# Five one-hot buffers, a peeled first pass, one block of counts turned per window, and weight splits between x1's low parts, in a two-layer graph kernel

## What is computed

```python
# layer 0, graph attention
h = x @ W
al, ar = h @ a_l, h @ a_r
e = exp(-leaky_relu(al[src] + ar[dst], 0.1))
h_prime = segment_sum(e[:, None] * h[dst], src) / (segment_sum(e, src)[:, None] + 1e-5)
x = layernorm(x + elu(h_prime))                       # called x1 below
# layer 1, relational convolution and gate
u = x @ root + bias
for r in range(8):
    mean = segment_sum(x[src] * (type == r), dst) / max(count, 1)
    u = u + mean @ weight[r]
z = concat([u, x]) @ w_gate + b_gate
out = layernorm(x + tanh(u) * z + x * (1 - z))
```

## Time and profile before

| what | us |
|---|---|
| median of 3 runs (1108.06 to 1109.21) | 1109.0 |
| the profiled execution, whole | 1109.11 |
| its span, first to last instruction | 1107.3 |
| TensorE busy in the span | 1042.9 (94%) |
| VectorE, ScalarE, GpSimd busy | 344.8, 275.4, 265.8 |
| mean granted TensorE clock | 0.977 of full |

### The profile page before, as it was taken

How to read it: one execution, slowest core, us unless ns; L and a number is a source line. 1 busy time by engine, 2 the same in 40 slices (tenths; PEclk the granted TensorE clock), 3 DMA queues, 4 the chain that set the end, 5 groups by cost and what they waited for, 6 DMA issues and landing times.

```text
span 1107.3 us, 14903 instructions
## 1 busy us (share of the span) xinstructions
PE 1042.9 (94%) x5430; PEld 857.2 (77%) x5430; DVE 344.8 (31%) x694; ACT 275.4 (25%) x470; POOL 265.8 (24%) x201
## 2 busy tenths in 40 slices
PE   5899879996999999999999999999999999999977
PEld 3566546775889889879889879889889889888855
DVE  7976765360112202202202102102102202112277
ACT  4322343383112212212212211211212211212320
POOL 0000000106331321221321321321321321327480
PEclk9999999998999999999999999999999998999989
DMA  6213335407321041041141141141141140212212
GB/s 209 76 39 108 94 96 152 133 28 262 122 76 39 30 147 37 29 146 37 31 145 38 29 146 30 38 145 34 33 146 38 30 147 28 75 48 67 76 39 92
DMA packets 63622, 91.81 MB, mean 83 GB/s; under 512 B 4116, under 2 KB 30179, under 8 KB 63429
## 3 DMA queue, kind: packets, MB, share of 16 engines
q1 hardware_dynamic: 63556, 90.86, 26.4%
HBM read 75.17 MB, written 15.67 MB: 82 GB/s over the span
## 4 chain that ended last, share of the span: by engine, by line
PE 84%; DVE 7%; POOL 3%; issue 3%; ACT 2%; DVEq 1%; DMA 0%; SPq 0%; ACTq 0%; POOLq 0%
PE ps L966 18%; PE ps L968 17%; PE ps L967 17%; PE ps L1154 9%; PE ps L1155 9%; PE ps L1030 4%; PE ps L993 2%; PE ps L1143 2%; DVE hot L790 2%; DVE oh_s L722 2%; POOL x_lo L426 1%; PE ps L1203 1%; POOL u L411 1%; PE ps L1205 1%; PE ps L1204 1%
## 5 line engine op out<-in xcount | busy, mean ns | idle before, releaser
L399 POOL TENSOR_TENSOR w_lo<-w_raw,w_hi 128x512 fp32r<-128x512 f32 x168 | 215.8, 1288 | 761.7 <-ACT w_hi L465 562.7
L966 PE MATMUL ps<-w_hi,M_hi 128*128 128x512 f32 (+1 forms) x560 | 223.4, 399 | 17.4 <-POOL w_lo L399 9.4
L465 ACT CAST w_hi<-w_raw 128x512 fp32r<-128x512 f32 x184 | 114.4, 622 | 498.2 <-PE ps L968 430.8
L968 PE MATMUL ps<-w_lo,M_hi 128*128 128x512 f32 (+1 forms) x560 | 219.7, 392 | 0.0
L967 PE MATMUL ps<-w_hi,M_lo 128*128 128x512 f32 (+1 forms) x560 | 219.7, 392 | 0.0
L883 DVE SCALAR_TENSOR_TENSOR u<-ps,scale,u 128x512 f32<-128x512 f32 (+1 forms) x90 | 66.4, 744 | 427.7 <-PE ps L968 427.7
L1154 PE MATMUL ps<-C_hi,x_hi 128*128 128x320 f32 (+3 forms) x640 | 194.0, 320 | 0.0
L1155 PE MATMUL ps<-C_hi,x_lo 128*128 128x320 f32 (+3 forms) x640 | 193.0, 318 | 0.0
L966 PE MATMUL ps<-w_hi,M 128*128 128x512 f32 (+1 forms) x360 | 142.9, 397 | 0.0
L967 PE MATMUL ps<-w_hi,M 128*128 128x512 f32 (+1 forms) x360 | 142.6, 396 | 0.0
L968 PE MATMUL ps<-w_lo,M 128*128 128x512 f32 (+1 forms) x360 | 142.3, 395 | 0.0
(11 more groups left out here) (145 smaller groups left out, 773.2 us busy)
## 6 DMA issues: line engine op xcount, KB each, us to landing
w_raw<-weights SPq DMA_DIRECT2D x192, 256.0 KB, 2.9
C_dram<-Cst SPq DMA_DIRECT2D x25, 512.0 KB, 6.0
C_hi<-C_dram SPq DMA_DIRECT2D x8, 1600.0 KB, 7.4
z<-b_gate SPq DMA_DIRECT2D x5, 512.0 KB, 9.8
u<-bias SPq DMA_DIRECT2D x5, 512.0 KB, 7.6
xT_raw<-xT SPq DMA_DIRECT2D x8, 312.5 KB, 7.5
u<-x SPq DMA_DIRECT2D x4, 512.0 KB, 5.2
out<-u SPq DMA_DIRECT2D x4, 512.0 KB
```

The lines of the kernel that those rows point to most:

```text
L399: pool.tensor_tensor(w_lo[k % RING][:, :], w_raw[k % RING][:, :], w_hi[k % RING][:, :].bitcast(f32), ALU.subtract).then_inc(w_lo_done, 1)
L465: nc.scalar.copy(w_hi[k % RING][:, :], w_raw[k % RING][:, :]).then_inc(w_hi_done, 1)
L966: mm(o, lhs_hi[:, k, c], w_hi[k % RING][:, :], start=opens, stop=False)
L968: last = mm(o, lhs_hi[:, k, c], w_lo[k % RING][:, :], start=False, stop=closes_)
```

## The change

Five buffers for the one-hots; the first pass of each window written out ahead of the loop, which then holds the further passes (a window of one pass skips it); the first counting matmul of a window opens the bank itself, and one tiny matmul instead of two closes it; the blocks of `turn_counts` one in each of the windows 8j+8 to 8j+12, with their copies in the windows of blocks 3 and 4; a ring of three for `att16`, which makes room for the fifth buffer; and in the z product another order of splits and loads on GpSimd, ScalarE and SyncE. The core of the diff:

```diff
-    SLOT = [0, 1, 2, 0, 3]
-    SLOTS = 1 + max(SLOT)
+    RING_A = 3
-            att16 = sb("att16", [P, NT, NP], i16, early)
-            hot = sb("hot", [P, SLOTS * NP], bf16, early)
+            att16 = sb("att16", [P, RING_A, NP], i16, early)
+            hot = sb("hot", [P, BODY * NP], bf16, early)
@@ sync
             flush(NT - 1)
+            for k in range(RING):
+                load_chunk(SEG_Z, k + RING)
             sp.wait_ge(y_sq_done, NT)
             sp.wait_ge(flushed[NT - 1], 16 * NT)
             load_counts(0)
             sp.wait_ge(turned, 2 * NT)
             for t in range(NT):
                 sp.dma_start(z[:, t, :], b_gate.partition_broadcast(P)).then_inc(z_here, 16)
-            load_ahead(SEG_Z)
+            for k in range(RING):
+                load_chunk(SEG_Z + 1, k)
             sp.wait_ge(x1T_ready, NT)
             sp.wait_ge(x1_lo_done, NT)
@@ gpsimd
-            for t in range(NT):
+            def x1_low(t):
                 pool.wait_ge(x1_hi_done, t + 1)
                 pool.tensor_tensor(x1_lo[0:rows(t), t, :], ...
-            split_ahead(SEG_Z)
+            split_chunk(SEG_Z, RING)
+            split_chunk(SEG_Z, RING + 1)
+            x1_low(0)
+            split_chunk(SEG_Z, RING + 2)
+            x1_low(1)
+            split_chunk(SEG_Z, RING + 3)
+            x1_low(2)
+            split_chunk(SEG_Z + 1, 0)
+            x1_low(3)
+            split_chunk(SEG_Z + 1, 1)
+            x1_low(4)
+            split_chunk(SEG_Z + 1, 2)
+            split_chunk(SEG_Z + 1, 3)
             split_ahead(SEG_Z + 1)
@@ scalar
+                if j >= RING_A:
+                    act.wait_ge(att_done, j - RING_A + 1)
-                        if w == PER * j + 10 + 2 * part:
+                        if w == PER * (j + 1) + (PART_A - 1 if part == 0 else NT - 1):
                             copy_turned(j, part)
...
-            split_ahead(SEG_Z)
+            x1_high(0)
+            split_chunk(SEG_Z, RING)
+            x1_high(1)
+            split_chunk(SEG_Z, RING + 1)
+            x1_high(2)
+            split_chunk(SEG_Z, RING + 2)
+            x1_high(3)
+            split_chunk(SEG_Z, RING + 3)
+            x1_high(4)
+            for k in range(RING):
+                split_chunk(SEG_Z + 1, k)
             split_ahead(SEG_Z + 1)
@@ vector
+            def hots(w, i):
+                dve.reg_add(turn, turn, 1)
+                n = dve.snap(turn, min_val=1, max_val=WINDOWS * ALL_TILES)
+                tile = dve.snap(i % STARTS)
+                for s in range(BODY):
+                    dve.wait_ge(counted[s], n)
+                    v.tensor_scalar(hot[:, s * NP:(s + 1) * NP], ...).then_inc(built[s], 1)
             for w in range(WINDOWS):
                 first_pass = window_range(DVE_ENGINE, w)
-                with dve.Fori(first_pass, LOOP_END, STARTS + BODY) as i:
+                hots(w, first_pass)
+                with dve.Fori(first_pass + (STARTS + BODY), LOOP_END, STARTS + BODY) as i:
+                    hots(w, i)
@@ tensor
+            def counts(w, i, first):
+                pe.reg_add(turn, turn, 1)
+                n = pe.snap(turn, min_val=1, max_val=WINDOWS * ALL_TILES)
+                edge = pe.snap((i % STARTS) * P)
+                if first:
+                    pe.wait_ge(window_copied, w + 1)
+                for s in range(BODY):
+                    pe.wait_ge(built[s], n)
+                    for c in range(2):
+                        last = mm(bank(5 + c, c=SPLIT), oh_s[:, ds(edge + s * P, P)],
+                                  hot[:, s * NP + c * SPLIT:s * NP + (c + 1) * SPLIT],
+                                  start=first and s == 0, stop=False, skip_group_check=True)
+                    last.then_inc(counted[s], 1)
             for w in range(WINDOWS):
                 first_pass = window_range(PE_ENGINE, w)
-                pe.wait_ge(window_copied, w + 1)
-                for c in range(2):
-                    mm(bank(5 + c, c=2), zeros[:, :], zeros[:, 0:2], start=True, stop=False, skip_group_check=True)
-                with pe.Fori(first_pass, LOOP_END, STARTS + BODY) as i:
+                counts(w, first_pass, True)
+                with pe.Fori(first_pass + (STARTS + BODY), LOOP_END, STARTS + BODY) as i:
+                    counts(w, i, False)
-                for c in range(2):
-                    last = mm(bank(5 + c, c=2), zeros[:, :], zeros[:, 0:2], start=False, stop=True, ...)
-                last.then_inc(window_counted, 1)
+                mm(bank(6, c=2), zeros[:, :], zeros[:, 0:2], start=False, stop=True, skip_group_check=True)\
+                    .then_inc(window_counted, 1)
                 for k, t in items(w):
                     xw_item(1, k, t)
                 for j in range(NT - 1):
-                    for ahead, part, blocks in ((8, 0, (0, 1)), (9, 0, (2, 3)), (11, 1, (4,))):
-                        if w == PER * j + ahead:
-                            turn_counts(j, part, blocks)
+                    m = w - PER * (j + 1)
+                    if 0 <= m < NT:
+                        turn_counts(j, 0 if m < PART_A else 1, (m,))
```

More of the change, by code:

```diff
@@ L506, in copy_turned @@
                 act.wait_ge(turned, 2 * j + part + 1)
-                nc.scalar.copy(att16[:, j, m0 * P:m1 * P], bank(turn_bank(j, part), c=(m1 - m0) * P)).then_inc(turned_read, 1)
+                if j >= RING_A:
+                    act.wait_ge(att_done, j - RING_A + 1)
+                nc.scalar.copy(att16[:, j % RING_A, m0 * P:m1 * P], bank(turn_bank(j, part), c=(m1 - m0) * P)).then_inc(turned_read, 1)
             def add_ar(j):
@@ L598, in _, with x1_high @@
             x1T_high(4)
-            for t in range(NT):
+            def x1_high(t):
                 nc.scalar.copy(x1_hi[0:rows(t), t, :], u[0:rows(t), t, :]).then_inc(x1_hi_done, 1)
-            split_ahead(SEG_Z)
+            x1_high(0)
[9 more added lines that the diff above has]
+                split_chunk(SEG_Z + 1, k)
             split_ahead(SEG_Z + 1)
@@ L778, in att_low @@
                  .then_inc(attT_lo_done, 1)
+            dve.wait_ge(oh_done, KT)
             turn = dve.alloc_register("dve_turn")
             dve.reg_mov(turn, 0)
+            def hots(w, i):
[4 more added lines that the diff above has]
+                    dve.wait_ge(counted[s], n)
+                    v.tensor_scalar(hot[:, s * NP:(s + 1) * NP], table[:, :], float(WIN * w),
+                                    key[:, ds(tile + s, 1)], ALU.add, ALU.is_equal).then_inc(built[s], 1)
             for w in range(WINDOWS):
                 first_pass = window_range(DVE_ENGINE, w)
-                with dve.Fori(first_pass, LOOP_END, STARTS + BODY) as i:
[L785 to L791, removed]
+                hots(w, first_pass)
+                with dve.Fori(first_pass + (STARTS + BODY), LOOP_END, STARTS + BODY) as i:
+                    hots(w, i)
                 for k in range(RING - 1, KT):
@@ L950, in _ @@
             for s in range(BODY):
-                if SLOT_BEFORE[s] >= s:
-                    pe.sem_inc(counted[SLOT_BEFORE[s]], 1)
+                pe.sem_inc(counted[s], 1)
             pe.wait_ge(units_diag_done, 1)
@@ L1017, in _ @@
             pe.reg_mov(turn, 0)
+            def counts(w, i, first):
[11 more added lines that the diff above has]
+                    last.then_inc(counted[s], 1)
             for w in range(WINDOWS):
                 first_pass = window_range(PE_ENGINE, w)
-                pe.wait_ge(window_copied, w + 1)
-                for c in range(2):
-                    mm(bank(5 + c, c=2), zeros[:, :], zeros[:, 0:2], start=True, stop=False, skip_group_check=True)
-                with pe.Fori(first_pass, LOOP_END, STARTS + BODY) as i:
[L1024 to L1028, removed]
-                        for c in range(2):
-                            last = mm(bank(5 + c, c=SPLIT), oh_s[:, ds(edge + s * P, P)],
-                                      hot[:, SLOT[s] * NP + c * SPLIT:SLOT[s] * NP + (c + 1) * SPLIT],
-                                      start=False, stop=False, skip_group_check=True)
-                        last.then_inc(counted[s], 1)
-                for c in range(2):
-                    last = mm(bank(5 + c, c=2), zeros[:, :], zeros[:, 0:2], start=False, stop=True, skip_group_check=True)
-                last.then_inc(window_counted, 1)
+                counts(w, first_pass, True)
[3 more added lines that the diff above has]
+                    .then_inc(window_counted, 1)
                 for k, t in items(w):
```

3 lines of the change are left out of this document (1 added, 2 removed).

## The result

After the change the kernel takes 1153.41 us (median of 4, 1150.99 to 1155.17); the kernel before, beside it, 1108.53 (median of 4). The ratio is 1.0403, with a 95% interval of 1.038 to 1.0426. The forecast was 1083. The profiled execution of after took 1154.4 us, its span is 1152.5, and its mean clock 0.973 against 0.977.

What follows compares the result with a forecast made beforehand. It took TensorE's path, 84% of the chain, as the bound. Savings of 21.5 us in the window stage and 4.8 in the z product, 26.3 off 1109.11, gave about 1083 us, range 1073 to 1094.

Steps and rivals of the forecast that it cites:

- the skip branch: Window loop: 38 windows jump over their loop on both engines, costed at nothing, with 0.2 us a window as bound.
- Rival D: Window loop: the skip lands beyond TensorE's fetched instructions, 118 us slower, total about 1201; chance 0.04.
- rival E: The change doesn't do what it says: one-hots still wait, z gives its 12 us back, total 1109; chance 0.02.
- cast 24 to 31: Windows 24 to 31: 19.5 us instead of 24.59, 5.1 saved.
- window stage, saved: All forty windows: 21.5 us saved, from 13 if VectorE or a sequencer paces them to 23 without a copy in the way.
- stall behind the bias: z product, second half's chunk 4: queued behind the bias broadcasts, it makes TensorE stall for a new 5.6 us.
- z stretch, saved: z product: 12.1 us saved, less 5.6 of new stall and 1.7 of clock, net 4.8, between 2 and 10.
- casts of windows 12 and 16 four times 2.86 apart: Sign in the window stage: each of these four windows takes 2.86 us, where it took 3.28.
- The price of the bias at 410 GB/s: z product: the bias's 2.56 MB at 410 GB/s, 6.2 us after a start-up of 2, would make the stall 1.9.
- Rival B: z product: the bias hides, so the z product gives 10 to 12 us, total 1076; chance 0.17.
- Rival C: Window stage: VectorE paces windows, each 0.2 to 0.25 us longer; the stage gives 13, total 1091; chance 0.19.
- The step on the moved copy: Windows 19 to 31: ScalarE's earlier copy delays the cast of h about 1 us, and window 27 by 0.5.

Runs made afterwards that it cites:

- e2: The kernel after, with a test around the loop of further passes on both engines so that 38 windows really skip it: 1084.07 us, ratio 0.9786.
- e3: The kernel after, with only the head of TensorE's relation loop aligned to start a block of 256 instructions: 1137.87 us, ratio 1.0263.
- e9: The kernel before, with only the head of TensorE's relation loop put 20 instructions ahead of a block's end: 1124.73 us, ratio 1.0148.
- e8: e5 with ScalarE's copy of the turned blocks moved to the end of its work in a window: 1070.55 us, ratio 0.9658.
- e1: The kernel after, with the first pass back inside the loop and the opening pair of tiny matmuls back: 1087.35 us, ratio 0.9829.
- e10: e8 with a hint for the jump back of TensorE's relation loop: 1068.0 us.
- e5: e2 with loads of chunks 4 to 7 of the z product's second half ahead of the bias broadcasts on SyncE's queue: 1073.11 us, ratio 0.9698.

## Why the prediction was wrong

**The step that failed** is the one on the skip branch: "Each of 38 windows now jumps over its loop on both engines." None does. The compare stands at the end of the body, and a loop entered with its variable already at or behind its end runs once. Two things ahead of the prediction said so. The section on the kernel states that the loop runs at least once, and the section on the change then says that a window of one pass skips it, which was never held against the first. And the earlier trace rows count it: 42 branches of the window loop for 42 passes. A loop with a test at its entry too would show 40 more. I read that row for its 67 and 228 ns, and not for its x42. The same row of after, on TensorE's sequencer:

```profile
L1068 PEldq COMPARE_BRANCH  x40: 74/74/97, 51.3 to 230.5; - x40
```

Forty branches, one behind each further pass, and none taken, at most 97 ns. The cost is the distance between the last casts of after and e2, 230.99 - 180.85 = 50.1 us for 38 passes, 1.32 each (1.35 where nothing else hides it). Less the gain of 201.30 - 180.85 = 20.5 that is there all the same, that is the +29.7.

**The second failed step** is an edit that the prediction did not list: the code ahead of the relation loop grew, and its head came to lie elsewhere. The unchanged loop was costed at nothing by silence. It lost 19.5 us. The three gaps are 13.7 of it. Behind each, ten matmuls take 510.12 - 506.24 = 3.9 us at a granted clock of about half, where ten at 0.23 apart take 2.3: 1.6 lost, 4.8 for three. The waits for M_lo grew by 1.0, and the sum is 19.5. The cause of this part is shown both ways, by e3 and e9.

**Rival D** named the right place with the wrong mechanism. It had the skip as the one way to a slower kernel, through the price of a far jump; e2 shows that the jump, once it exists, costs 0.21 us and is hidden. Its chance of 0.04 was the price of jumps alone. That the loop is not skipped at all, which comes under "the change doesn't do what it says", was only thought of for the buffers, in rival E.

**The rest of the sum held**, as e2 shows term by term:

| step | worked out | e2 |
|---|---|---|
| plain window | 2.86 | 2.88 |
| cast 0 to cast 19 | 64.3 | 64.1 |
| cast 19 to cast 24 | 16.5 | 16.8 |
| cast 24 to 31 | 19.5 | 20.6 |
| cast 31 to 39 | 29.0 | 29.0 |
| window stage, saved | 21.5 | 20.5 |
| stall behind the bias | 5.6 | 6.24 |
| z stretch, saved | 4.8 | 3.5 |
| total | 1083 | 1084.07 |

Windows 24 to 31 are off by 1.1 us, and it is the moved copy that was sized too small there: the plain step, 25 to 26, takes 137.22 - 134.74 = 2.48 (worked out: 2.59), and e8, which moves the copy alone, takes the stretch to 19.6. The z stretch is off by 1.3, of which 0.6 is the longer stall. The sign "casts of windows 12 and 16 four times 2.86 apart" was itself wrong: they are 103.36 - 91.03 = 12.33 apart in e2, 3.08 a window, because the new order puts a block of counts (0.87) into window 12; without it four times 2.86 are left. The price of the bias at 410 GB/s comes out as 1.3 from its own terms (273.4 + 2 + 6.2 + 0.6 + 2 - 282.9), and not as 1.9.

In after itself the z product follows the same steps, 29.7 us later: chunk 4 of the first half begins at 285.34 without the stall of 9.43 (forecast 255.6 + 29.7 = 285.3), the bias is issued at 303.62 (303.1), and chunk 4 of the second half begins at 318.98 (318.2).

**Rival B** (the bias hides) is out by the 6.14 and 6.24 of idle time. **Rival C** (VectorE's sequencer paces the windows) is out by the 2.88 and by the 20.5 of the stage, where it would give 13. The step on the moved copy has the right mechanism and too small a size: 1 us of delay in windows 19 to 24 and 0.5 in window 27 were forecast, and e8 gets 1.8 and 1.0 back.

The rule of the Trainium skill, page "Runtime: NRT & Kernel Launch", section "Instruction fetch mechanics", that a taken branch beyond the fetched window waits for the fetch of its target, agrees with the far jump (3.4 us) and is not touched by the near one (0.21). The same section says that instructions come in blocks of 256; e3 and e9, which place the head by that figure, bear it out. The traces show more: a head near a block's end paid twice, for the jump's own 3.7 us (`L1200 PEldq COMPARE_BRANCH  x4: 83/3734/3771, 495.5 to 1017.0; - x4` in after) and for the gap of 4.9 a few matmuls later. The rule on taken branches alone makes no difference between after and before here.

**What is settled, and what stays open.** The z stretch is 107 in e1 and e3 and 103.3 to 103.9 in after and e2, with idle times of 6.1 to 6.3 in all four. The first 12 us of it, in e1 and then in e2, tell the difference:

```profile
182.00:194.00 12.00, 11.26 (x59) 10.41 (x60) 1.65 (x2) 2.91 (x5) 4.96 (x4) 0.72 0.88 239
```

```profile
180.85:192.85 12.00, 11.26 (x74) 10.20 (x75) 1.65 (x2) 2.90 (x5) 4.97 (x4) 1.00 0.88 238
```

TensorE is as busy in both, but in e1 the granted clock is 0.72, and 28% of 12 us are the 3 us that are missing; e3 shows 0.72 in its first 12 us too, and after 1.00. With full clock there e1 and e3 would show the gain of the z product as well. Why the clock falls there in some executions stays open, as does the clock in the relation steps (790 to 800 us in kernels without the gap).

## What to carry to other kernels

Before writing the first pass of a loop out ahead of it, ask whether the loop can run no times: divide the number of its branches in the trace by the number of passes, and if it is one per pass, guard what is left with a condition (0.21 us here, hidden) or leave it alone (2.4 us to be had here). After any edit, count the instructions of each group against what the data ask for; an x that doubled says more than any time. When a stretch without an edit becomes slower, look behind its loop's jump for idle time ended by "issue": here the place of the code was the cause, and an aligned head removed the gap (e3). A hint shortened the jump itself (e10); it was not tried on a kernel with the gap.

## What the runs showed of the hardware that I had not expected

- A jump back whose head lies shortly before the end of a block of instructions costs a second stop: 4.4 us (e9) and 4.9 us (after) of idle TensorE, 17.7 and 19.5 us in all for three jumps, since the clock falls behind each. That after's head lies there is inferred, as said at e9. In the stretches below, of after, TensorE does nothing for 4 us while the core's DMA engines are full (share 1.03, 396 GB/s); whether the fetch is slow because of that load was not tried.

```profile
502.00:506.00 4.00, 0.00 (x0) 0.00 (x0) 0.00 (x0) 0.00 (x0) 0.00 (x0) 1.00 1.03 396
506.00:510.00 4.00, 3.76 (x10) 2.87 (x10) 0.00 (x0) 0.02 (x1) 0.00 (x0) 0.58 0.30 109
```

- A hint ahead of a far jump takes it from 3.3 to 3.7 us (e8) down to 0.22 (e10), for 34 ns of TensorE's sequencer each.
- Five broadcasts of a row into 128 partitions, queued ahead of a 128 x 512 weight chunk, hold it back by 316.97 - 303.62 = 13.4 us in after, from the first broadcast's issue to the chunk's cast. The same bytes behind the chunks cost nothing that can be seen (e5).

The best version is e10: five buffers, the first pass written out with a true skip, blocks spread, the copy last, the chunks ahead of the bias, and the hint. It takes 1068.0 us, 3.5% less than before (interval of the ratio 0.9622 to 0.9675) and about 7% less than after.
